# The upper adjacency quarters issued from GpSimd's queue instead of ScalarE's

## The chip, the cores and the metric

One core of a Trainium2 chip runs the whole program. The metric is device time in microseconds, lower is better. The engines are TensorE (PE), VectorE (DVE), ScalarE (ACT), GpSimd (POOL) and SyncE (SP); each works through its own instructions in order, and semaphores order them against each other. DMAs are issued from the queues of SyncE, ScalarE and, after the change, GpSimd.

## What is computed

Two graph layers with a residual and a layer norm each, on 10000 nodes with 128 features, all in float32:

```python
h = item_feat @ W_item.T + b_item
x = layernorm(x + relu(adj @ h + x @ W_user.T + b_user))      # adj is 10000 x 10000, 400 MB
Wh = x @ W
e = leaky_relu(Wh @ a[:128] + (Wh @ a[128:]).T, 0.2)
att = softmax(where(adj > 0, e, -9e15), axis=1)
x = layernorm(x + elu(att @ Wh))
```

## The kernel before

**Two parts.** The first part reads the adjacency once, 400 MB, computes layer 1 and stores the signs of the adjacency as one bit each (`mask_scratch`). The second part computes layer 2 from the bits. The change is in the first part, up to about 1650 us.

**Tiling of the first part.** The 10000 rows are 19 blocks of 512 (`IB`) and a last one of 272; `k` counts them. The 10000 columns are 10 chunks (`NC`) of 1024 (`JC`), the last of 784; `c` counts them. A chunk of a block is loaded in two halves of 256 rows (n = 2c and 2c + 1), so a block has 20 halves. A half lies in one of five slots (`RAW`) of the buffer `raw`: the 128 partitions are four quarters `a` of 32 (`Q`), each with 256 of the 1024 columns, and partition i of a quarter holds rows i, 32 + i, 64 + i and so on. A DMA fills one quarter of one half: 32 partitions x 8 rows x 1 KiB, 256 KB. So a half takes four DMAs and a block 80.

**Who does what with it.** SyncE issues quarters 0 and 1 (`load_half`, L356), ScalarE quarters 2 and 3 (`load_upper`, L979). Both wait for the same count of `half_turned`, the transpose that frees the slot five halves back, and both raise `adj_loaded[slot]`. VectorE waits for all four quarters and transposes the half into `adj_t` (`half_transposed`, L691). When both halves of a chunk are turned, TensorE contracts it with eight matmuls of 512 columns (`contract`, L573), and ScalarE takes the sign (`mask_chunk`, L1011), which VectorE packs by eights (L736, L742, L750). `adj_t` has two chunks, so VectorE may be at most two chunks ahead of TensorE.

**ScalarE's order before.** For each chunk of a block: `loads_ahead` issues the upper quarters of halves 2c + 5 and 2c + 6, then `mask_chunk(c)`; between them, at fixed chunks, come the small steps of the block before: relu (L1032), the copy of x (L1038), deviations (L1045), the store of x1 (L1050), the copy of x1 (L1058), scores (L1068) and their store, which writes single words (L1072), and the mask stores (L1017). Before the first block ScalarE turns the item features (L992) and issues the first upper quarters at chunks 5, 7 and 9 of that loop and behind it.

**GpSimd's order before.** Constants at the start, then one copy per block (`keep_x1`, L458), which waits for ScalarE's copy of x1 (`x1_turned_sb`). In the second part it computes an epilogue per block (L295, L307).

**Loops.** Blocks 0 to 2 are written out, blocks from 3 on run in a hardware loop of two blocks a turn, the last ones are written out again.

Of the kernel before, what the change touches and what calls it, by code (L numbers as in the profile page):

```python
# [50 lines left out]
def resnorm_two_graph_layers(nc, x, adj, item, w_item, b_item, w_user, b_user, w_att, a_att, out):  # L51
# [25 lines left out]
    def cols_of(c):  # L77
        return JA if c < NC - 1 else LJ

    with ExitStack() as ctx:  # L80
# [3 lines left out]
        def sem(name):  # L84
            return ctx.enter_context(nc.semaphore(name))
# [94 lines left out]
        padding_cleared = sem("padding_cleared")  # L180
        adj_loaded = [sem(f"adj_loaded{i}") for i in range(RAW)]
        half_turned = sem("half_turned")
        chunk_contracted = sem("chunk_contracted")
# [250 lines left out]
        def _(pool):  # L434
# [16 lines left out]
            last_chunk = x1_t[:, (NC - 1) * JC:NC * JC]  # L451

            def keep_x1(k, par, width, first):

# [14 lines left out]

            blocks(pool, keep_x1)  # L470
            pool.wait_ge(x1_plain_made, 2)
# [196 lines left out]
        def _(dve):  # L668
# [7 lines left out]
            def half_transposed(k, n, width):  # L676

                c, half, slot = n // 2, n % 2, n % RAW
                steps = steps_of(c)
                groups = HG if half == 0 or width == IB else width // Q - HG  # L680
                off = 0 if c < NC - 1 else LOFF

                uses = k * (2 * NC // RAW) + n // RAW + 1
                dve.wait_ge(adj_loaded[slot], uses * (16 * A))
                if half == 0 and not (isinstance(k, int) and k * NC + c < 2):
                    dve.wait_ge(chunk_contracted, k * NC + c - 1)
                    dve.wait_ge(mask_made, k * NC + c - 1)
# [272 lines left out]
        def _(act):  # L960
            def load_upper(k, n, width):

                c, half = n // 2, n % 2
                slot = n % RAW
                groups = HG if half == 0 or width == IB else width // Q - HG
                rows = Q if half == 0 or width == IB else TAIL - HG * Q - (groups - 1) * Q
                off = 0 if c < NC - 1 else LOFF
                if not (isinstance(k, int) and k * 2 * NC + n < RAW):
                    act.wait_ge(half_turned, k * (2 * NC) + n - RAW + 1)
                for a in (2, 3):  # L970
                    cols = slice(c * JC + a * cols_of(c), c * JC + (a + 1) * cols_of(c))
                    if rows == Q:
                        src = adj[bass.ds(k * IB + half * HG * Q, groups * Q), cols].rearrange("(g i) w -> i g w", i=Q)
                        dst = raw[a * Q:(a + 1) * Q, slot, 0:groups, off:off + cols_of(c)]
                    else:
                        assert groups == 1
                        src = adj[N - rows:N, cols]
                        dst = raw[a * Q:a * Q + rows, slot, 0, off:off + cols_of(c)]
                    act.dma_start(dst, src).then_inc(adj_loaded[slot], 16)  # L979

            for c in range(NC):
                n = min(N, (c + 1) * JC) - c * JC
                if c >= 5 and (c - 5) // 2 < RAW and c % 2 == 1:
                    load_upper(0, (c - 5) // 2, IB)
                act.wait_ge(item_turned, c + 1)
# [15 lines left out]

            for n in range(NC // 2 - 2, RAW):
                load_upper(0, n, IB)

            def mask_chunk(k, c, width):
# [7 lines left out]
            def store_masks(k, half, width):  # L1013
# [4 lines left out]
                              packed[:, half, 0:HC * width // 4]).then_inc(masks_stored[half], 16)  # L1018

            def loads_ahead(k, c, nxt):  # L1020

                for n in (2 * c + RAW, 2 * c + 1 + RAW):
                    if n < 2 * NC:
                        load_upper(k, n, IB if nxt else TW)
                    elif nxt:
                        load_upper(k + 1, n - 2 * NC, nxt)

# [45 lines left out]

            def layer1(k, par, width, first, nxt=IB):
# [22 lines left out]

            layer1(0, 0, IB, True)
            layer1(1, 1, IB, False)
            layer1(2, 0, IB, False)  # L1100
            with act.Fori(3, NB - 3, 2) as k:
                layer1(k, 1, IB, False)
                layer1(k + 1, 0, IB, False)
            layer1(NB - 2, 1, IB, False)
            layer1(NB - 1, 0, IB, False, TW)
            layer1(NB, 1, TW, False, 0)

# [104 lines left out]
```

## Time and profile before

| | us |
|---|---|
| three runs | 3139.74, 3150.01, 3197.87 |
| median | 3150.01 |
| the profiled execution | 3156.98 |
| its span in the trace | 3155.2 |

The profile is one execution. Its page gives busy time and instructions of each engine, the same in 40 slices of the span (79 us each), the DMA queues, the chain of work that ended last (followed back from the last instruction, at each step to what released it), and the costliest groups of instructions by line. PE and DVE overlap, so their shares don't add. "q1" is SyncE's DMA queue and "q10" ScalarE's. ACTq, SPq and POOLq mean the queue of the engine: issuing a DMA, arithmetic on registers. "issue" is time in which an engine waited for nothing that the profile shows. A line such as L979 is the line of the kernel that made the instruction. The DMA share of a window can exceed 1, since packets of one engine overlap.

### The profile page before, as it was taken

The page shows a single profiled execution, that of the slowest core. Times are in us where ns is not written, and L with a number is a line of the kernel's source. Part 1 is how long each engine was busy: PE and PEld are TensorE (multiplying, and loading weights), DVE is VectorE, ACT ScalarE, POOL GpSimd, SP SyncE. Part 2 cuts the span into 40 slices and gives each one's busy share as a digit, 9 for nine tenths or more (in the row PEclk, how much of TensorE's full clock was granted, in tenths as well). Part 3 has the DMA queues.
Part 4 walks back from the last instruction along what each step waited for, and adds up shares of the span by engine and source line. Part 5 has one row for each costly group of instructions (what it writes and reads, how often), then busy time and mean ns, then how long its engine had stood idle before and what let it go on. Part 6 is the DMA issues. An engine that isn't in the chain of part 4 may idle for free.

```text
span 3155.2 us, 50455 instructions
## 1 busy us (share of the span) xinstructions
PE 2947.8 (93%) x16484; PEld 2121.8 (67%) x16484; DVE 2646.8 (84%) x3522; ACT 861.7 (27%) x506; POOL 246.6 (8%) x186
## 2 busy tenths in 40 slices
PE   8999998888997889899997999999999999999998
PEld 5444443343443334344477999999999999999995
DVE  5888876676775677677779999999999999999995
ACT  3555444344443344444441100000000000000000
POOL 0000000000000000000003111112111111111120
PEclk9999999999999999899998999999999999999999
DMA  9999999999999999999971000000000000000000
GB/s 268 314 302 300 286 272 247 233 250 246 277 271 217 230 263 270 237 275 271 264 176 60 12 19 21 19 15 15 18 15 15 15 15 15 15 23 15 15 7 9
DMA packets 498749, 457.98 MB, mean 145 GB/s; under 512 B 39744, under 2 KB 490992, under 8 KB 498544
## 3 DMA queue, kind: packets, MB, share of 16 engines
q1 hardware_dynamic: 248352, 233.87, 30.2%
q10 hardware_dynamic: 250320, 223.28, 29.1%
q8 instruction: 24, 0.39, 0.1%
q14 instruction: 53, 0.43, 0.1%
HBM read 433.81 MB, written 23.22 MB: 145 GB/s over the span
## 4 chain that ended last, share of the span: by engine, by line
PE 60%; DMA 18%; ACTq 8%; DVE 8%; issue 4%; ACT 1%; DVEq 0%; SPq 0%
PE bank L631 42%; DMA area<-in_adj_dram 18%; PE bank L573 17%; ACTq L979 7%; DVE area L691 3%; DVE area_s L844 2%; DVE unpacked L902 1%; PE bank L598 0%; ACTq L1017 0%; DMA area_x<-in_L_gnn_item_feat_dram 0%; ACT area_m L1011 0%; PE bank L510 0%; PE bank L552 0%; ACT area L1123 0%; DVEq L924 0%
## 5 line engine op out<-in xcount | busy, mean ns | idle before, releaser
L631 PE MATMUL bank<-area_h,area_s 128*128 (+2 forms) x12482 | 1443.6, 277 | 47.2 <-DVE area_s L844 47.2
L573 PE MATMUL bank<-area,area_h 128*128 128x512 f32 (+1 forms) x3160 | 1396.9, 600 | 86.0 <-DVE area L691 85.5
L631 PEld LDWEIGHTS bank<-area_h,area_s 128*128 128x128 f32 (+1 forms) x12482 | 1405.9, 191 | 83.6 <-issue 72.0
L691 DVE STREAM_TRANSPOSE area<-area 128x2048 f32<-128x2048 f32 (+3 forms) x400 | 894.1, 2235 | 376.9 <-DMA area<-in_adj_dram 270.3
L844 DVE SCALAR_TENSOR_TENSOR area_s<-area,c_col,unpacked 128x512 f32<-128x512 uint8 (+2 forms) x1580 | 1170.3, 801 | 37.9 <-PE bank L631 26.2
L573 PEld LDWEIGHTS bank<-area,area_h 128*128 128x128 f32 x3160 | 609.8, 196 | 817.2 <-issue 719.5
L1011 ACT ACTIVATE area_m<-area 128x4096 uint8<-128x4096 f32 (+1 forms) x200 | 700.1, 3501 | 853.5 <-issue 582.4
L1171 ACT ACTIVATE std_o<-mv,eps_col 128x4 f32<-128x4 f32 (+1 forms) x20 | 6.0, 298 | 929.2 <-DVE mv L869 929.2
L902 DVE TENSOR_TENSOR unpacked<-area,bit_of 128x1024 uint32<-128x1024 uint32 (+1 forms) x200 | 246.1, 1231 | 0.0
L736 DVE SCALAR_TENSOR_TENSOR packing<-area_m 128x512 uint32<-128x512 uint32 (+1 forms) x200 | 134.0, 670 | 38.6 <-ACT area_m L1011 38.5
L458 POOL COPY area_x<-area_s 128x512 f32 (+1 forms) x19 | 11.7, 613 | 1603.8 <-ACT area_s L1058 1603.8
L295 POOL TENSOR_TENSOR area<-wh_mean,den 128x512 f32<-128x512 f32 x19 | 19.8, 1042 | 1158.8 <-DVE den L857 1158.8
L742 DVE SCALAR_TENSOR_TENSOR packing<-packing 128x256 uint32<-128x256 uint32 (+1 forms) x200 | 75.3, 377 | 0.0
L1158 ACT COPY area<-bank 128x258 f32<-128x258 f32 (+1 forms) x40 | 12.9, 375 | 210.1 <-PE bank L631 210.1
L1164 ACT ACTIVATE area<-area 128x512 f32<-128x512 f32 (+1 forms) x20 | 12.5, 625 | 172.9 <-POOL area L307 171.0
L750 DVE SCALAR_TENSOR_TENSOR packed<-packing 128x128 uint32<-128x128 uint32 (+1 forms) x200 | 49.7, 249 | 0.1
L552 PEld LDWEIGHTS bank<-w_ts,area_s 128*128 128x128 f32 (+1 forms) x158 | 23.5, 220 | 35.1 <-ACT area_s L1058 30.4
L552 PE MATMUL bank<-w_ts,area_s 128*128 128x2 f32 (+1 forms) x158 | 23.1, 267 | 23.5 <-ACT area_s L1058 23.5
L535 PE MATMUL bank<-ident,area_s 128*128 128x128 f32 (+1 forms) x79 | 14.3, 309 | 27.8 <-DVE area_s L695 27.7
L307 POOL TENSOR_SCALAR area<-area 128x512 f32<-128x512 f32 x19 | 38.2, 2012 | 0.0
L535 PEld LDWEIGHTS bank<-ident,area_s 128*128 128x128 f32 (+1 forms) x79 | 9.9, 153 | 41.0 <-DVE area_s L695 39.6
L1113 ACT COPY area_h<-bank 128x387 f32<-128x387 f32 (+1 forms) x27 | 12.6, 474 | 88.9 <-PE bank L598 88.9
(102 smaller groups left out, 674.3 us busy)
## 6 DMA issues: line engine op xcount, KB each, us to landing
area<-in_adj_dram SPq DMA_DIRECT2D x702, 256.0 KB, 8.3
area<-in_adj_dram ACTq DMA_DIRECT2D x702, 256.0 KB, 10.5
area<-in_adj_dram SPq DMA_DIRECT2D x78, 196.0 KB, 6.9
area<-in_adj_dram ACTq DMA_DIRECT2D x78, 196.0 KB, 8.4
mask_scratch<-packed ACTq DMA_DIRECT2D x38, 320.0 KB, 13.1
area<-mask_scratch SPq DMA_DIRECT2D x19, 640.0 KB, 3.9
x_scratch<-area_s ACTq DMA_DIRECT2D x20, 256.0 KB, 14.6
area<-x_scratch SPq DMA_DIRECT2D x20, 256.0 KB, 2.8
```

Of the source, the lines that this page charges most:

```text
L307: ops.tensor_scalar(el[:, 2, 0:w], el[:, 0, 0:w], 0.0, -1.0, ALU.max, ALU.add).then_inc(elu_halves, 1)
L552: mm = nc.tensor.matmul(ps_ts[0:m, 2 * t:2 * t + 2], x1_blk[:, t * P:t * P + m], w_ts[:, :], start=True, stop=True)
L573: mm = nc.tensor.matmul(acc[par][:, 0:width], h[:, c * SPC + s, :], adj_t[:, c % 2, s * width:(s + 1) * width], start=(c == 0 and s == 0), ...
L631: mm = nc.tensor.matmul(bank[0:m, (t % 2) * DEN:(t % 2 + 1) * DEN], prob[:, slot, t * P:t * P + m], right, start=start and t % 2 == 0, sto ...
L691: nc.vector.transpose(dst, src).then_inc(half_turned, 1)
L736: nc.vector.scalar_tensor_tensor(out=packs[:, 0:4, 0:w], in0=m[:, 0:4, :], scalar=4, in1=m[:, 4:8, :], op0=ALU.logical_shift_left, op1=ALU ...
L742: nc.vector.scalar_tensor_tensor(out=packs[:, 4:6, 0:w], in0=packs[:, 0:2, 0:w], scalar=2, in1=packs[:, 2:4, 0:w], op0=ALU.logical_shift_l ...
L750: nc.vector.scalar_tensor_tensor(out=packed[:, c // HC, (c % HC) * w:(c % HC + 1) * w], in0=packs[:, 4, 0:w], scalar=1, in1=packs[:, 5, 0: ...
L844: nc.vector.scalar_tensor_tensor(out=prob[:, slot, 0:width], in0=lhs, scalar=scalar, in1=mask, op0=ALU.max, op1=ALU.mult).then_inc(weights ...
L902: nc.vector.tensor_tensor(unpacked[:, slot, 0:n, 0:w], src.bitcast(U32)[:, None, :].to_broadcast([P, n, w]), bit_of[:, 0:n, None].to_broad ...
L979: act.dma_start(dst, src).then_inc(adj_loaded[slot], 16)
L1011: nc.scalar.activation(mask_out[:, c % 2, 0:w], adj_t[:, c % 2, 0:w], ACT.Sign).then_inc(mask_made, 1)
```

## The change

`load_upper` and `loads_ahead` move from ScalarE's program to GpSimd's. GpSimd now walks through the blocks chunk by chunk: two halves' upper quarters, and the copy of x1 of the block before at chunk 6. The first five halves wait for the item chunks (`item_turned` 2, 4 and 6 for halves 0, 1 and 2). The upper quarters raise a semaphore of their own, `upper_loaded[slot]`, and VectorE waits for both. ScalarE's walk loses `loads_ahead` and nothing else.

```diff
+        upper_loaded = [sem(f"upper_loaded{i}") for i in range(RAW)]
...
+            def load_upper(k, n, width):
...
+                if not (isinstance(k, int) and k * 2 * NC + n < RAW):
+                    pool.wait_ge(half_turned, k * (2 * NC) + n - RAW + 1)
+                for a in (2, 3):
...
+                    pool.dma_start(dst, src).then_inc(upper_loaded[slot], 16)
...
-            blocks(pool, keep_x1)
+            def layer1(k, par, width, nxt=IB):
+                first = isinstance(k, int) and k == 0
+                for c in range(NC):
+                    loads_ahead(k, c, nxt)
+                    if c == at(6) and not first:
+                        keep_x1(k - 1, 1 - par, IB, False)
+
+            for n in range(RAW):
+                if n < NC // 2 - 2:
+                    pool.wait_ge(item_turned, 2 * n + 2)
+                load_upper(0, n, IB)
+            layer1(0, 0, IB)
...
+            with pool.Fori(3, NB - 3, 2) as k:
+                layer1(k, 1, IB)
+                layer1(k + 1, 0, IB)
...
+            keep_x1(NB, 1, TW, False)
...
-                dve.wait_ge(adj_loaded[slot], uses * (16 * A))
+                dve.wait_ge(adj_loaded[slot], uses * 32)
+                dve.wait_ge(upper_loaded[slot], uses * 32)
...
-            def load_upper(k, n, width):
...
-                    act.dma_start(dst, src).then_inc(adj_loaded[slot], 16)
...
-                if c >= 5 and (c - 5) // 2 < RAW and c % 2 == 1:
-                    load_upper(0, (c - 5) // 2, IB)
...
-            for n in range(NC // 2 - 2, RAW):
-                load_upper(0, n, IB)
...
-                    loads_ahead(k, c, nxt)
...
+            blocks(act, layer1)
```

## Rows read from the trace of the kernel before

**Rows 1.** The page: rate in 40 slices, adjacency transposes, ScalarE's issues.

```profile
GB/s 268 314 302 300 286 272 247 233 250 246 277 271 217 230 263 270 237 275 271 264 176 60 12 19 21 19 15 15 18 15 15 15 15 15 15 23 15 15 7 9
...
L691 DVE STREAM_TRANSPOSE area<-area 128x2048 f32<-128x2048 f32 (+3 forms) x400 | 894.1, 2235 | 376.9 <-DMA area<-in_adj_dram 270.3
...
area<-in_adj_dram ACTq DMA_DIRECT2D x702, 256.0 KB, 10.5
```

**Rows 2.** The page: the chain that ended last, by line.

```profile
PE bank L631 42%; DMA area<-in_adj_dram 18%; PE bank L573 17%; ACTq L979 7%; DVE area L691 3%; DVE area_s L844 2%; DVE unpacked L902 1%; PE bank L598 0%; ACTq L1017 0%; DMA area_x<-in_L_gnn_item_feat_dram 0%; ACT area_m L1011 0%; PE bank L510 0%; PE bank L552 0%; ACT area L1123 0%; DVEq L924 0%
```

**Rows 3.** Windows: stretch, length, busy us by engine, TensorE clock, DMA share, GB/s.

```profile
110.00:366.00 256.00, 256.00 (x651) 117.10 (x651) 216.50 (x244) 137.47 (x57) 1.87 (x3) 1.00 1.10 308
...
1000.00:1500.00 500.00, 449.12 (x1070) 201.12 (x1069) 356.75 (x391) 221.50 (x89) 3.67 (x6) 0.95 1.10 256
```

**Rows 4.** GpSimd in order of time: start, length, line, operation, idle before.

```profile
153.34 0.63 POOL L458 COPY area_x<-area_s 128x512 f32<-128x512 f32 x1 [149.75 <-ACT area_s L1058]
...
366.59 0.61 POOL L458 COPY area_x<-area_s 128x512 f32 x1 [70.15 <-ACT area_s L1058]
449.28 0.61 POOL L458 COPY area_x<-area_s 128x512 f32 x1 [82.08 <-ACT area_s L1058]
...
1562.41 0.61 POOL L458 COPY area_x<-area_s 128x512 f32 x1 [79.71 <-ACT area_s L1058]
```

**Rows 5.** Chain by line, from 200 to 400, then 1000 to 1100 us.

```profile
by line: PE bank L573 87.8%; DMA area<-in_adj_dram 8.3%; PE bank L571 1.3%; PE bank L552 1.2%; DVE area L691 1.0%; issue 0.7%; PE bank L543 0.7%; PE bank L535 0.5%; PE bank L561 0.4%; DVE packing L736 0.3%; ACTq L979 0.3%
...
by line: DMA area<-in_adj_dram 70.3%; ACTq L979 22.3%; DVE area L691 7.0%; issue 5.7%; ACTq L1017 1.9%; ACTq L1050 1.6%; ACTq L1072 0.5%; ACT area_m L1011 0.2%; ACTq L969 0.2%; ACT ts_col L1068 0.2%; ACTq L1008 0.1%; ACTq L1006 0.1%; ACTq L
```

**Rows 6.** Waits (total, times, longest), 110 to 360, then 500 to 1500 us.

```profile
DVE area L691 <- DMA area<-in_adj_dram: 2.1, 4, 1.3
...
DVE area L691 <- DMA area<-in_adj_dram: 221.8, 138, 6.4
```

**Rows 7.** Source lines: L979 110 to 360, L979 and L356 500 to 1500.

```profile
L979 ACTq DMA_DIRECT2D area<-in_adj_dram x142: 317/384/3231, 111.1 to 359.2; - x142
...
DMA to landing us min/median/max: 4.5/9.3/14.8
...
L979 ACTq DMA_DIRECT2D area<-in_adj_dram x467: 318/1287/6768, 502.5 to 1496.6; - x156
...
  DVE area L691: 218.5, 133
...
DMA to landing us min/median/max: 4.3/11.8/20.5
...
L356 SPq FUSED_REGOPS  x470: 37/37/51, 500.9 to 1499.5; - x157
...
L356 SPq DMA_DIRECT2D area<-in_adj_dram x470: 316/317/4917, 501.1 to 1499.7; - x157
...
  DVE area L691: 4.5, 4
...
DMA to landing us min/median/max: 4.4/8.1/18.8
```

**Rows 8.** DMA queues in the microsecond from 1010, then from 852.

```profile
DMA packets 230, 0.23 MB, mean 228 GB/s; under 512 B 14, under 2 KB 229, under 8 KB 229
...
q1 hardware_dynamic: 17, 0.02, 8.4%
...
DMA packets 364, 0.35 MB, mean 352 GB/s; under 512 B 20, under 2 KB 364, under 8 KB 364
...
q1 hardware_dynamic: 179, 0.17, 53.6%
```

**Rows 9.** Source lines L295 and L307.

```profile
L295 POOL TENSOR_TENSOR area<-wh_mean,den x19: 1041/1041/1043, 1764.3 to 3069.0; 128x512 f32<-128x512 f32 x19
...
L307 POOL TENSOR_SCALAR area<-area x19: 1977/2013/2017, 1770.2 to 3074.3; 128x512 f32<-128x512 f32 x19
```

**Rows 10.** TensorE in order of time: the first contraction.

```profile
43.98 7.13 PE L573 MATMUL bank<-area,area_h 128*128 128x512 f32 x16 [1.29 <-DVE area L691]
```

More of the change, by code:

```diff
@@ L451, in _, with loads_ahead @@
             last_chunk = x1_t[:, (NC - 1) * JC:NC * JC]
+            def load_upper(k, n, width):
+                c, half = n // 2, n % 2
+                slot = n % RAW
+                groups = HG if half == 0 or width == IB else width // Q - HG
+                rows = Q if half == 0 or width == IB else TAIL - HG * Q - (groups - 1) * Q
+                off = 0 if c < NC - 1 else LOFF
+                if not (isinstance(k, int) and k * 2 * NC + n < RAW):
+                    pool.wait_ge(half_turned, k * (2 * NC) + n - RAW + 1)
+                for a in (2, 3):
+                    cols = slice(c * JC + a * cols_of(c), c * JC + (a + 1) * cols_of(c))
+                    if rows == Q:
+                        src = adj[bass.ds(k * IB + half * HG * Q, groups * Q), cols].rearrange("(g i) w -> i g w", i=Q)
+                        dst = raw[a * Q:(a + 1) * Q, slot, 0:groups, off:off + cols_of(c)]
+                    else:
+                        assert groups == 1
+                        src = adj[N - rows:N, cols]
+                        dst = raw[a * Q:a * Q + rows, slot, 0, off:off + cols_of(c)]
+                    pool.dma_start(dst, src).then_inc(upper_loaded[slot], 16)
+            def loads_ahead(k, c, nxt):
+                for n in (2 * c + RAW, 2 * c + 1 + RAW):
+                    if n < 2 * NC:
+                        load_upper(k, n, IB if nxt else TW)
+                    elif nxt:
+                        load_upper(k + 1, n - 2 * NC, nxt)
             def keep_x1(k, par, width, first):
@@ L468, in keep_x1 @@
                     nc.gpsimd.tensor_copy(x1_plain[:, IB:IB + width], x1_blk[:, 0:width]).then_inc(x1_kept, 1)
-            blocks(pool, keep_x1)
+            def layer1(k, par, width, nxt=IB):
[9 more added lines that the diff above has]
+            layer1(0, 0, IB)
+            layer1(1, 1, IB)
+            layer1(2, 0, IB)
+            with pool.Fori(3, NB - 3, 2) as k:
+                layer1(k, 1, IB)
+                layer1(k + 1, 0, IB)
+            layer1(NB - 2, 1, IB)
+            layer1(NB - 1, 0, IB, TW)
+            layer1(NB, 1, TW, 0)
+            keep_x1(NB, 1, TW, False)
             pool.wait_ge(x1_plain_made, 2)
@@ L960, in _ @@
         def _(act):
-            def load_upper(k, n, width):
[L963 to L978, printed above, removed]
-                    act.dma_start(dst, src).then_inc(adj_loaded[slot], 16)
             for c in range(NC):
                 n = min(N, (c + 1) * JC) - c * JC
-                if c >= 5 and (c - 5) // 2 < RAW and c % 2 == 1:
-                    load_upper(0, (c - 5) // 2, IB)
                 act.wait_ge(item_turned, c + 1)
@@ L1018, in store_masks @@
                               packed[:, half, 0:HC * width // 4]).then_inc(masks_stored[half], 16)
[L1020 to L1026, printed above, removed]
             def relu(k, par, width):
@@ L1072, in scores_out, with layer1 @@
                     act.dma_start(s_dram[:, bass.ds(k * IB, IB)].rearrange("o (t p w) -> p (o t) w", p=P, w=1), ts_col[:, :, 1:2]).then_inc(s_stored_dram, 16)
-            def layer1(k, par, width, first, nxt=IB):
+            def layer1(k, par, width, first):
                 live = width if width == IB else TAIL
@@ L1096, in layer1 @@
                         store_masks(k, 0, width)
[L1098 to L1106, printed above, removed]
+            blocks(act, layer1)
             def wh_copied(lo, hi):
```

## The prediction

> **What bounds the kernel now.** I read the page first [rows 1, 2]. The kernel has two parts. In the first, up to about 1650 us, the DMA row is full and the adjacency streams in at 210 to 310 GB/s; in the second the rate is about 15 GB/s and TensorE works without a break. The diff touches only the first. In the chain of work that ended last, L631, L844 and L902 are the second part (45% of the span together); what is left is TensorE at L573 (17%), landings of adjacency (18%) and ScalarE's queue issuing L979 (7%). So the first part has two bounds in turn, and the question is when each holds.
>
> The windows say when [rows 3]. From 110 to 366 us TensorE is busy for all 256 us, at full clock, and DMA moves 308 GB/s. From 1000 to 1500 us TensorE is busy for 449 of 500 us, at 0.95 of its clock, and DMA moves 256 GB/s. GpSimd's one copy per block is a ruler for the block period [rows 4]: it makes 19 of them; from the first, at 153.34, to the fourth, at 366.59, a block takes 71.1 us, and from there to the eighteenth, at 1562.41, 85.4 us. The difference is 14.3 us per block, 14 x 14.3 = 201 us in all, and that is all that this change can give back, since the first spell is already bound by TensorE: its chain is 87.8% L573 [rows 5]. In the later spell the chain has no TensorE in it: 70.3% is landings and 22.3% L979 on ScalarE's queue.
>
> Who is late? VectorE's transposes (L691) wait for adjacency 2.1 us in the early 250 us and 221.8 us in the later 1000 us [rows 6]. Of the later wait 218.5 us are owed to DMAs issued by L979, the upper quarters from ScalarE, and 4.5 us to L356, the lower quarters from SyncE [rows 7], though both are asked for by the same semaphore and have the same shape. L979's issue has also grown: median 384 ns early, 1287 ns later, up to 6768 ns, while L356 stays at 317 ns. ScalarE issues four of them per chunk between two mask instructions. Their landing is later too, 11.8 us against 8.1.
>
> The bandwidth is not simply used up. In one microsecond where the upper queue is nearly alone (17 of 230 packets are the lower queue's) 228 GB/s move; in one where the two have equal shares, 352 [rows 8]. The queues feed the two halves of the partitions, and when they take turns instead of overlapping, a third of the rate is lost. A late upper half makes them take turns.
>
> **The change part by part.** (a) *ScalarE loses its adjacency issues*: 780 full-size ones [rows 1] and 20 small ones of the last block. On its queue remain the mask instructions, the stores and the small copies. Nothing of this is on the early chain; in the later spell it is the 22.3%. ScalarE's masks come no later than now.
>
> (b) *GpSimd gains the same 800 issues* and waits for the same count of `half_turned`. What stands before it there: one copy per block (0.61 us, [rows 4]), placed after the loads of chunk 6. It waits for ScalarE's copy of x1, which stands at chunk 5 in ScalarE's own order, before the half that the next load waits for is turned, so I cost it at 0.6 us per block, hidden. If that cover went, the loads of chunk 7 would be late, and L691 behind them.
>
> (c) *The price of one issue on GpSimd*, t, decides the case, and no row shows it: GpSimd issues no DMA in this trace. GpSimd must get through 40 issues per block, so 40t is a third bound beside TensorE's 71.1. Lower end: 0.32 us, the same transfer from SyncE [rows 7]. Upper end: if GpSimd builds the 256 pieces of a transfer (32 partitions x 8 rows of 1 KiB) one by one in software, each on a reading and a writing side, its slowest pass over 512 elements, 2.01 us (L307 [rows 9]), is the nearest row for 512 such steps; with ScalarE's 0.38 us for the issue itself, 2.4 us. Between them I take GpSimd's faster pass over 512 elements, 1.04 us (L295 [rows 9]), plus 0.38: t = 1.4 us, so 40t = 57 us, hidden under TensorE's 71.1. Cover ends at t = 71.1/40 = 1.78 us. A slot of the ring of five lives 5 x 3.55 = 17.8 us at the early pace; less a transpose of 2.2 us [rows 1], 15.6 us are left for two issues (2.8) and a landing (9.3 [rows 7]), 12.1 in all: early enough.
>
> [...]
>
> (d) *The separate semaphore* adds one wait in front of each of 400 transposes. SyncE's register step takes 37 ns [rows 7], so some 40 ns each, 16 us over the kernel, on a VectorE that is busy 216 of 256 us while TensorE is the bound [rows 3]: nothing, and 16 us without that cover.
>
> (e) *The first five halves* go out from the second item chunk on instead of from the sixth. They take bandwidth from the item tiles: 0.5 MB at 308 GB/s is 1.7 us for each of three. Against that, block 0 finds its halves landed. I cost it at 0, with 5 us either way.
>
> **The sum**, on the profiled execution (span 3155.2 us, 3157.0 with what lies around it; the median of the runs is 3150.0, 0.2% lower). Best case: every block takes 71.1 us, 3155 - 201 = 2954. I don't expect all of it. The pace changes between the copies at 366.59 and 449.28 us [rows 4], where the code does nothing new; whatever tips it there can tip a kernel with better ordered loads too. If one block in five still runs at the later pace, 0.2 x 201 = 40 us stay: 2995 us, 5% less than now. Parts (a) to (e) add nothing else.
>
> **The rivals.** *A, the forecast*: punctual upper loads, t below 1.78, most blocks at TensorE's pace: 2995, within 2954 and 3060.
>
> *B, nothing that can be measured*: the 16 DMA engines are one pool, and lateness on L979 is a symptom: its issue takes long because the engines are behind. For it: the DMA share is 1.10 in both spells [rows 3], so the engines have work at all times. Then the queues go on taking turns under another name, and only the issue share is partly won: 3100 to 3170, middle 3140. Against it: that SyncE's twin transfers are almost never waited for. [...] The equal share of 1.10 agrees with it; the step from 228 to 352 GB/s with the mixture of the two queues doesn't.
>
> *C, GpSimd becomes the bound (slower)*: one mechanism, 40t above the present period. If t is above 1.78 every full block takes 40t. There are 14 of them at 85.4 us, and 4.6 from 44 to 366.6 us at 71.1, so the time is 3155 + 14(40t - 85.4) + 4.6(40t - 71.1) = 1632 + 744t. It breaks even at t = 2.05, is 2% slower from 2.13 and 2% faster below 1.96. At the upper end, 2.4, it is 3418. For it: two software issues must fit into every 3.55 us, and GpSimd's slower pass over 512 elements already says 2.4. Against it: only that the faster pass says 1.4. [...]
>
> *D, a third queue upsets the sharing (slower)*: GpSimd's transfers come late in the turn of each DMA engine behind SyncE's, at t far below 1.78. Each block would then run at the one-queue rate: 20.5 MB per block at 228 GB/s is 90 us, 14(90 - 85.4) + 4.6(90 - 71.1) = 151, so 3306.
>
> **How the numbers follow.** A 0.43, B 0.19, C 0.33, D 0.05. C is high because t is a guess between 0.32 and 2.4 with the edges at 1.96 and 2.13. Of C, 0.04 falls between these edges. Faster by over 2% (below 3087): 0.43. Within 2%, which is about what a measurement of this kernel tells from no change: 0.19 + 0.04 = 0.23. Slower (over 3213): 0.29 + 0.05 = 0.34. The time is that of A, 2995. The range reaches from the full gain, 2950, to C's upper end, 3420; above it I leave some 0.12 for a t beyond 2.4, below it 0.02. Both signs are inside; A's own range is 2954 to 3060.
>
> **What the profile after would show.** For A: full blocks at 71 to 75 us by GpSimd's copies, L691's wait for adjacency small for both queues, TensorE's clock near 1.0, over 290 GB/s. For B: periods of 83 to 86 us, and the wait of L691 as large as before but owed to GpSimd's line. For C: the GpSimd queue issuing without a gap from the first block, the issues two by two per transpose, and a constant block period of 40 times their mean, in the early blocks too. For D: short issues on GpSimd but landings well above 12 us. The forecast is wrong if the mean issue is above 1.78 us, or if L979's slowness was a symptom; (b) is wrong if the copy's wait has a load queued behind it that VectorE waits for; (e) if TensorE's L573 begins more than 5 us from 44 us [rows 10].

## The result and the profile after

| | us |
|---|---|
| after, three runs | 3406.12, 3406.65, 3409.51 |
| after, median | 3406.65 |
| span of the profiled execution | 3407.8 |
| before, median | 3150.01 |
| ratio after to before | 1.0835, 95% interval 1.0791 to 1.0879 |

The change makes the kernel 8% slower: 252.6 us from span to span. The ratios here and below leave out runs that are over 1.5% slower than the fastest of the same kernel (here 3197.87 us of the kernel before). These lines of the page of the kernel after answer to [rows 1, 2]: rate in 40 slices (now 85 us each), the queues (packets, MB, share of 16 engines' span), the chain that ended last, two groups of instructions, and the issues with their median time to landing. L741 is now the adjacency transpose, L472 GpSimd's load, L357 SyncE's, L622 the contraction, L487 GpSimd's copy of x1.

```profile
GB/s 219 243 231 232 228 235 232 239 236 219 224 217 229 224 232 214 235 230 231 226 229 224 89 12 14 14 22 17 17 14 14 17 21 14 17 14 14 18 9 8
...
q1 hardware_dynamic: 248352, 233.87, 34.0%
q0 software_dynamic: 61792, 200.05, 25.1%
...
PE bank L680 38%; DMA area<-in_adj_dram 34%; SPq L357 7%; DVE area L741 4%; PE bank L622 4%; DVE area_s L894 3%; DVE unpacked L952 1%; SPq L365 1%; DMA area_x<-in_L_gnn_item_feat_dram 1%; PE bank L647 0%; DVE packing L786 0%; PE bank L559 0%; ACT area L1131 0%; PE bank L584 0%; PE bank L550 0%
...
L741 DVE STREAM_TRANSPOSE area<-area 128x2048 f32<-128x2048 f32 (+3 forms) x400 | 894.5, 2237 | 653.2 <-DMA area<-in_adj_dram 568.3
...
L472 POOL DMA_DIRECT2D area<-in_adj_dram x800 | 466.8, 585 | 1390.2 <-DVE area L741 1276.8
```

The 300 GB/s of the early slices are gone; it is about 230 from the first slice to the end of the first part. In the chain the contraction has shrunk from 17% to 4%, landings have grown from 18% to 34%, and the issue queue in it is no longer ScalarE's (L979, 7%) but SyncE's (L357, 7%), a line the change did not touch. The transposes wait 568.3 us for adjacency, before 270.3. And q0, GpSimd's queue, moves 200 MB in 61792 packets: for the full transfers it puts four 1-KiB pieces into one packet of 4096 bytes (44928 such packets, 64 for each of 702 transfers; 12800 of the rest are of 4 bytes), where q1 has one packet for each piece (180000 of 1024 bytes).

The windows of the kernel after (stretch, length, busy us by engine, TensorE's granted clock, DMA share, GB/s; compare [rows 3]) and GpSimd's copies of x1, the 1st, 4th and 18th (compare [rows 4]):

```profile
110.00:366.00 256.00, 215.12 (x493) 95.18 (x494) 165.68 (x187) 106.18 (x42) 66.32 (x114) 0.92 1.08 234
...
1000.00:1500.00 500.00, 408.56 (x940) 180.81 (x939) 315.79 (x350) 195.46 (x79) 124.94 (x213) 0.91 1.07 227
```
```profile
193.37 0.62 POOL L487 COPY area_x<-area_s 128x512 f32<-128x512 f32 x1
...
471.09 0.62 POOL L487 COPY area_x<-area_s 128x512 f32 x1
...
1807.39 0.62 POOL L487 COPY area_x<-area_s 128x512 f32<-128x512 f32 x1
```

The first copy comes 40.0 us later than before, the next three blocks take 92.6 us each in place of 71.1 (+64.5), the next fourteen 95.5 in place of 85.4 (+140.5): 245 of the 252.6 us. So both spells of before are lost, the fast one more: even in the early window TensorE is busy for only 215 of 256 us. Of the first 40 us, 12.3 are the start (point e below).

The waits from 500 to 1500 us (compare [rows 6]), and the two loading lines in that stretch (duration ns min/median/max; compare [rows 7]), first SyncE's, then GpSimd's:

```profile
DVE area L741 <- DMA area<-in_adj_dram: 328.4, 127, 12.2
```
```profile
L357 SPq DMA_DIRECT2D area<-in_adj_dram x420: 316/786/12421, 498.9 to 1496.3; - x140
...
  DVE area L741: 325.0, 128
...
DMA to landing us min/median/max: 4.8/15.1/26.4
...
L472 POOL DMA_DIRECT2D area<-in_adj_dram x416: 586/586/600, 510.3 to 1496.9; - x139
...
DMA to landing us min/median/max: 5.3/8.7/16.2
```

The roles are swapped. Before, the upper quarters were waited for (218.5 us) and SyncE's hardly (4.5). Now SyncE's are waited for (325.0 us) and GpSimd's never. GpSimd's issue is short and steady, 0.586 us; it spends its time waiting for slots. It is SyncE's issue that has grown, 317 to 786 ns at the median and up to 12.4 us, and its landing is 15.1 us. One microsecond of the kernel after, from 1015, by queue (compare [rows 8]):

```profile
DMA packets 126, 0.25 MB, mean 253 GB/s; under 512 B 5, under 2 KB 84, under 8 KB 126
...
q0 software_dynamic: 46, 0.17, 68.7%
q1 hardware_dynamic: 80, 0.08, 36.4%
```

Both queues have work, and GpSimd's gets twice the bytes in fewer packets. By the program its packets go to the upper 64 partitions alone.

### The profile page after: what moved, and what is told of

It is laid out like the page before. It is cut to its first block, busy times and chain, and to the rows that moved or that the text cites. A ratio compares the mean times of both kernels' runs of the same rounds, so it can differ in the third digit from the quotient of the medians.

```text
span 3407.8 us, 50976 instructions
## 1 busy us (share of the span) xinstructions
PE 3022.4 (89%) x16484; PEld 2143.3 (63%) x16484; DVE 2648.7 (78%) x3522; ACT 861.8 (25%) x506; POOL 712.1 (21%) x986
## 3 DMA queue, kind: packets, MB, share of 16 engines
q0 software_dynamic: 61792, 200.05, 25.1%
## 4 chain that ended last, share of the span: by engine, by line
PE 43%; DMA 35%; DVE 10%; SPq 8%; issue 4%; ACT 1%; DVEq 0%; POOL 0%; ACTq 0%
PE bank L680 38%; DMA area<-in_adj_dram 34%; SPq L357 7%; DVE area L741 4%; PE bank L622 4%; DVE area_s L894 3%; DVE unpacked L952 1%; SPq L365 1%; DMA area_x<-in_L_gnn_item_feat_dram 1%; PE bank L647 0%; DVE packing L786 0%; PE bank L559 0%; ACT area L1131 0%; PE bank L584 0%; PE bank L550 0%
## 5 line engine op out<-in xcount | busy, mean ns | idle before, releaser
L622 PE MATMUL bank<-area,area_h 128*128 128x512 f32 (+1 forms) x3160 | 1470.0, 624 | 238.4 <-DVE area L741 238.1
L741 DVE STREAM_TRANSPOSE area<-area 128x2048 f32<-128x2048 f32 (+3 forms) x400 | 894.5, 2237 | 653.2 <-DMA area<-in_adj_dram 568.3
L622 PEld LDWEIGHTS bank<-area,area_h 128*128 128x128 f32 x3160 | 632.3, 204 | 1022.3 <-issue 783.9
L472 POOL DMA_DIRECT2D area<-in_adj_dram x800 | 466.8, 585 | 1390.2 <-DVE area L741 1276.8
L1172 ACT ACTIVATE area<-area 128x512 f32<-128x512 f32 (+1 forms) x20 | 12.5, 625 | 172.4 <-POOL area L308 170.5
L308 POOL TENSOR_SCALAR area<-area 128x512 f32<-128x512 f32 x19 | 38.2, 2011 | 0.0
L304 POOL TENSOR_SCALAR area<-area 128x512 f32<-128x512 f32 x19 | 32.8, 1727 | 3.1 <-POOL area L301 3.1
L819 DVE TENSOR_TENSOR area_h<-bank,b_item_row 128x512 f32<-128x512 f32 (+1 forms) x20 | 12.7, 677 | 26.3 <-PE bank L559 26.3
```

The lines of the kernel that those rows point to most:

```text
L308: ops.tensor_scalar(el[:, 2, 0:w], el[:, 0, 0:w], 0.0, -1.0, ALU.max, ALU.add).then_inc(elu_halves, 1)
L472: pool.dma_start(dst, src).then_inc(upper_loaded[slot], 16)
L622: mm = nc.tensor.matmul(acc[par][:, 0:width], h[:, c * SPC + s, :], adj_t[:, c % 2, s * width:(s + 1) * width], start=(c == 0 and s == 0), ...
```

## The experiments

In the order of the argument: first what makes the kernel after slow (e1 to e6, e11, e12), then what the later spell of before is (e7 to e10, e13). Ratios are to the kernel before, run beside each; its medians there were 3122 to 3148 us.

### Which partitions each queue fills (e1, e2, e3)

The first idea was that at each instant the two queues crowd into the same half of the partitions, so that giving each queue one quarter of either half would mend it. e1 crosses the quarters in the kernel after, e2 in the kernel before (the diff: SyncE's loop, then that of `load_upper`); e3 swaps the halves in the kernel after, SyncE (2, 3) and GpSimd (0, 1).

```diff
-                for a in (0, 1):
+                for a in (0, 2):
...
-                for a in (2, 3):
+                for a in (3, 1):
```

> The changed kernel, with one thing more: SyncE loads quarters 0 and 2, GpSimd 3 and 1, so each queue fills both halves of the partitions, and when the two are in step they write different halves. Theory 1 (ports and turns): a queue that fills 64 partitions can't pass some 210 GB/s, and GpSimd's 4096-byte packets take four times as much per turn as SyncE's 1024-byte ones, so the halves are filled one after the other. Crossing the quarters lifts the limit: TensorE's pace, 71 to 75 us per block, 2950 to 3050 us in all. Theory 2 (the software path is slow in itself, wherever it writes): nothing changes, 3350 to 3450 us.

> The kernel before, with SyncE loading quarters 0 and 2 and ScalarE 3 and 1. Theory 1: the later spell of 85 us per block goes too, since there the two queues also took turns on the halves: 2950 to 3000 us. Theory 2, under which the later spell came from ScalarE issuing late: 3100 to 3170 us, as before.

> The changed kernel with the halves swapped: SyncE loads quarters 2 and 3, GpSimd 0 and 1. Theory 1: no change, 3390 to 3430 us, and it is again SyncE's transfers that land late (15 us against 9). Theory 3 (the place matters: the upper partitions, or the place where GpSimd's descriptors lie): over 2% away from 3407, or GpSimd's transfers late.

e1: 3391.85 us, ratio 1.0875 (1.0776 to 1.0973). e2: 3324.22 us, ratio 1.0675 (1.0605 to 1.0746). e3: 3377.05 us in one run; GpSimd's landing 8.7 us and SyncE's 14.6, though SyncE now fills the upper half. So lateness goes with the queue and not with the place. The time of e3 is 13 us under the range of theory 1 and far from that of theory 3. Crossing doesn't mend the kernel after, against theory 1, and it spoils the kernel before, which neither theory had, in its early spell too:

```profile
110.00:366.00 256.00, 225.03 (x526) 100.17 (x525) 176.79 (x194) 113.06 (x45) 1.98 (x3) 0.94 1.11 254
```

(e2's window.) One queue on each half of the partitions is thus worth something, and the kernel after keeps that and loses it all the same.

### The loads alone (e4)

No computation: VectorE only frees the slots. Seven stages of 40 halves each, with the sources, slots and waits of the kernel:

```diff
+    STAGES = (
+        ("sp", (0, 1), None, ()),
+        ("sp", (0, 1), "act", (2, 3)),
+        ("sp", (0, 1), "pool", (2, 3)),
+        ("sp", (0, 2), "act", (3, 1)),
+        ("sp", (0, 2), "pool", (3, 1)),
+        ("sp", (), "pool", (2, 3)),
+        ("sp", (0, 2, 1, 3), None, ()),
+    )
```

> Leaves out the whole computation: seven stages of 40 halves each are loaded into a ring of five slots, VectorE reads each half once it has landed (about 2.2 us) and frees the slot; in the end x is copied to the output. Stages: SyncE 0,1 alone; SyncE 0,1 with ScalarE 2,3; SyncE 0,1 with GpSimd 2,3; SyncE 0,2 with ScalarE 3,1; SyncE 0,2 with GpSimd 3,1; GpSimd 2,3 alone; SyncE 0,2,1,3 alone. Theory 1: alone and on 64 partitions either queue gives 200 to 212 GB/s; SyncE with GpSimd on separate halves 225 to 250; the crossed pairs over 300. Theory 2: GpSimd alone well below SyncE alone (under 180), and the crossed pair with GpSimd no better than the separate one.

Its windows, one for each stage in that order (VectorE, GpSimd, clock, DMA share, GB/s):

```profile
18.00:103.00 85.00, 77.18 (x34) 0.00 (x0) 1.00 1.12 207
128.00:230.00 102.00, 77.06 (x34) 0.00 (x0) 1.00 1.09 343
263.00:402.00 139.00, 77.15 (x34) 35.80 (x62) 1.00 1.07 250
432.00:565.00 133.00, 76.88 (x34) 0.00 (x0) 1.00 1.12 263
600.00:743.00 143.00, 76.54 (x34) 35.89 (x62) 1.00 1.07 242
764.00:850.00 86.00, 76.68 (x34) 35.68 (x62) 1.00 1.03 203
882.00:1034.00 152.00, 77.72 (x34) 0.00 (x0) 1.00 1.14 239
```

Into 64 partitions either queue alone moves 203 to 207 GB/s: GpSimd's is as fast as SyncE's. Two hardware queues on the two halves reach 343, SyncE with GpSimd 250. The loss is there without any computation, and only in the pair, against theory 2, which had GpSimd alone under 180. But theory 1 had the crossed pairs over 300, and they move 263 and 242. So a limit of 64 partitions and turns between the queues isn't all of it. Why two hardware queues with equal packets move 343 on a half each and 263 crossed was not taken apart. The DMA share is above 1 in all seven stages, while the rate goes from 203 to 343: it tells that the engines have packets, not how much they move.

How the pair shares the engines stands in the packets themselves. One microsecond of the third stage, from 270, and one four later, from 274:

```profile
DMA packets 131, 0.26 MB, mean 262 GB/s; under 512 B 19, under 2 KB 83, under 8 KB 131
q0 software_dynamic: 64, 0.20, 74.1%
q1 hardware_dynamic: 67, 0.07, 29.7%
...
DMA packets 221, 0.21 MB, mean 212 GB/s; under 512 B 14, under 2 KB 221, under 8 KB 221
q1 hardware_dynamic: 221, 0.21, 111.3%
```

In the first microsecond, where both have work, they get about the same number of packets, 64 and 67, so GpSimd gets about three times the bytes (not four, since 19 of these packets have under 512 bytes). In the second GpSimd's part of a half is in, and SyncE moves the rest of its own alone at 212 GB/s, near the 207 of 64 partitions alone.

### The size of the pieces (e5)

If a DMA engine takes one packet from each queue in turn, as the equal counts above suggest, GpSimd's packet of 4096 bytes against SyncE's of 1024 gives the upper half 4/5 of what moves and the lower half 1/5. The halves are then filled one after the other, each near the 205 GB/s of 64 partitions, in place of both at once. e5 varies only the contiguous piece (KiB):

```diff
+        {"sp": ((0, 1), 1), "pool": ((2, 3), 1)},
+        {"sp": ((0, 1), 4), "pool": ((2, 3), 4)},
+        {"sp": ((0, 1), 4), "act": ((2, 3), 4)},
+        {"sp": ((0, 1), 4), "pool": ((2, 3), 1)},
+        {"sp": ((0, 1), 1), "act": ((2, 3), 4)},
+        {"sp": ((0, 1), 2), "pool": ((2, 3), 1)},
+        {"sp": ((0, 1), 1), "act": ((2,), 1), "pool": ((3,), 1)},
```

> Leaves out the whole computation, as the loads alone: seven stages of 40 halves, lower quarters by SyncE, upper ones by another queue, with contiguous pieces of 1, 2 or 4 KiB. Theory 1 in its present form (each DMA engine takes one packet from each queue in turn, and the 64-partition halves are filled evenly only if the packets are of one size): (1) SyncE 1 with GpSimd 1 KiB pieces, sent as 4096-byte packets: 249 GB/s as before; (2) SyncE 4, GpSimd 4: over 300; (3) SyncE 4, ScalarE 4: over 300; (4) SyncE 4, GpSimd 1: over 300; (5) SyncE 1, ScalarE 4, no software queue at all: 225 to 260; (6) SyncE 2, GpSimd 1: 260 to 290; (7) SyncE 1, ScalarE quarter 2, GpSimd quarter 3: 250 to 290. Theory 4 (a software queue disturbs the others whatever its packets): 2 and 4 stay near 250, and 5 is near 340.

```profile
32.00:172.00 140.00, 76.37 (x34) 35.15 (x61) 1.00 1.05 246
200.00:310.00 110.00, 76.89 (x34) 31.54 (x61) 1.00 1.03 316
338.00:451.00 113.00, 77.11 (x34) 0.00 (x0) 1.00 1.02 310
481.00:603.00 122.00, 76.13 (x34) 34.74 (x60) 1.00 1.03 284
637.00:773.00 136.00, 76.56 (x34) 0.00 (x0) 1.00 1.07 252
805.00:928.00 123.00, 76.29 (x34) 34.75 (x60) 1.00 1.04 276
961.00:1088.00 127.00, 76.03 (x34) 17.51 (x30) 1.00 1.11 274
```

The first, second and fifth lines decide. With 4-KiB pieces on both, SyncE and GpSimd reach 316, as much as two hardware queues with them (310). With 1 KiB on SyncE and 4 KiB on ScalarE, no software queue anywhere, it is 252. In its microsecond from 645 the two queues have 62 and 63 packets with 0.06 and 0.22 MB, the same sharing as GpSimd's. With loads alone it is the unequal packets that cost most of the rate, not the software queue. Not all: the fourth line has packets of 4096 bytes on both queues too, but GpSimd's are put together from 1-KiB pieces, and it moves 284, where over 300 was expected and the second line has 316. The median such packet of GpSimd takes 245 ns there and 207 ns in the second.

### Half of GpSimd's part back on ScalarE (e6)

```diff
-                for a in (2, 3):      # ScalarE's load_upper
+                for a in (2,):
...
+                for a in (3,):        # GpSimd's load_upper
```

> The changed kernel with quarter 2 back on ScalarE, so GpSimd loads one quarter of four. Theory 1: while GpSimd has work its packets take most of each turn, but for half as long: a block between 78 and 88 us, 3100 to 3300 us, between the two kernels, with SyncE's transfers landing later than 10 us. Theory 4: nearer to the changed kernel, 3300 to 3400 us.

3250.07 us, ratio 1.0441 (1.0265 to 1.0617), 256 GB/s from 110 to 366 us, 85.6 us a block over its first three and 86.8 over the next fourteen, SyncE's landing 13.9 us: all as theory 1 had it. Half the bytes in long packets cost about half, within a wide interval.

### Equal packets in the kernel after, unequal ones in the kernel before (e11, e12)

Here the piece size is changed inside the real kernels. e11 is the kernel after with 4-KiB pieces on both queues, e12 the kernel before with them on ScalarE's alone.

```diff
+                    if c < NC - 1 and groups == HG:
+                        src = adj[bass.ds(k * IB + (half * HG + 2 * a) * Q, 2 * Q), c * JC:(c + 1) * JC].rearrange("(g i) w -> i g w", i=Q)
+                        dst = raw[a * Q:(a + 1) * Q, slot, :, :].rearrange("p (g u) w -> p g (u w)", u=4)[:, :, 0:4 * JA]
```

> The kernel after, with the full halves of both queues in pieces of 4 KiB: each quarter takes 64 rows of the whole chunk in place of 256 rows of a quarter of it, the same 256 KB. The adjacency then lies wrong in the buffer, so the values are not those of the layers; every instruction and every byte is as in the kernel after, but for a few small memsets at the start. Theory 1 (a DMA engine takes one packet of each queue in turn, and only the unequal size, 1024 against 4096 bytes, starves SyncE's half): equal packets, at least 290 GB/s in the early blocks, landings within 2 us of each other, a block in 71 to 86 us, 2950 to 3200 us in all. Theory 4 (the software queue disturbs the other in itself): still about 230 GB/s and 90 us or more a block, 3300 to 3450 us.

> The kernel before, where only ScalarE's full halves come in pieces of 4 KiB (64 rows of a whole chunk for each quarter) and SyncE's stay at 1 KiB. The upper adjacency lies wrong in the buffer, so the values are not those of the layers. No software queue is used. Theory 1 (unequal packets): the slowness of the kernel after appears without GpSimd: about 230 to 255 GB/s from the first block on, 85 to 95 us a block, SyncE's landing later than ScalarE's, 3280 to 3420 us. Theory 4 (the software queue itself): like before, 3100 to 3200 us.

e11: 3185.38 us, ratio 1.0152 (1.0063 to 1.0242). e12: 3308.76 us, ratio 1.0559 (1.0462 to 1.0655). Windows from 110 and from 1000 us, first e11, then e12:

```profile
110.00:366.00 256.00, 244.06 (x611) 110.34 (x610) 201.97 (x220) 128.91 (x52) 73.96 (x140) 0.99 1.04 289
1000.00:1500.00 500.00, 421.02 (x998) 186.26 (x997) 335.10 (x371) 209.01 (x84) 122.50 (x229) 0.92 1.04 243
```
```profile
110.00:366.00 256.00, 220.83 (x527) 98.48 (x526) 174.52 (x192) 111.51 (x45) 1.98 (x3) 0.94 1.08 247
1000.00:1500.00 500.00, 420.50 (x982) 187.27 (x981) 327.88 (x358) 205.40 (x83) 3.04 (x5) 0.91 1.07 238
```

Equal packets bring the early blocks of the kernel after back to 289 GB/s; unequal ones take the early blocks of the kernel before down to 247, on hardware queues alone. With e13 (below) this makes a square:

| ratio to before | upper half on ScalarE | on GpSimd |
|---|---|---|
| packets equal | 0.9863 (e13, both 4 KiB) | 1.0152 (e11) |
| packets 1024 and 4096 bytes | 1.0559 (e12) | 1.0835 (after) |

Down a column, the unequal packets cost 0.070 and 0.068; along a row, GpSimd's queue costs 0.029 and 0.028. Each ratio is good to about 0.01, so that the two costs add is seen to within 0.02. The upper row has long pieces on both queues. From the kernel before itself, with 1 KiB on both, the way to the kernel after is 0.056 by unequal packets (e12) and 0.028 more by GpSimd's queue.

What makes up the 0.028 (its own 0.53 to 0.59 us an issue, a later start, packets put together from short pieces, or something else in the queue) was not taken apart. By GpSimd's copies e11 takes 74.9 us a block over its first three and 86.1 over the next fourteen, e13 78.0 and 77.7, so between these two it lies in the later spell; its first copy is 11.2 us later, of 111.8 us from span to span. Between the kernel after and e12 (88.6 and 90.2 us a block) it is 4.0 us a block early and 5.3 later. And equal packets don't make SyncE punctual beside GpSimd: in e11 its transfers land after 12.5 us (110 to 360 us) and 13.4 us (500 to 1500 us) at the median, against 10.1 for GpSimd's, more than the 2 us expected, and from 500 to 1500 us VectorE waits 230.3 us for them and 46.3 for GpSimd's.

The expectation of e12 also had SyncE's landing late. Its waits from 500 to 1500 us, first for SyncE's loads (L356), then for ScalarE's (L996):

```profile
L356 SPq DMA_DIRECT2D area<-in_adj_dram x443: 316/781/10305, 499.9 to 1498.0; - x148
...
  DVE area L705: 194.9, 89
...
L996 ACTq DMA_DIRECT2D area<-in_adj_dram x444: 322/352/5385, 499.9 to 1498.5; - x148
...
  DVE area L705: 122.9, 63
```

SyncE's issue grows as in the kernel after, with no GpSimd in it, and its landing is the later one from 110 to 360 us (12.0 against 9.5 at the median). But from 500 us on the landings are alike (8.4 and 8.3), and ScalarE's are waited for too, where GpSimd's in the kernel after never were. So e12 has the loss, and the roles less clearly. One caution more: its upper half reads its rows from other places of the adjacency than that of the kernel after.

### The later spell of the kernel before (e7, e8, e10, e9, e13)

The prediction lived on the drop from 71.1 to 85.4 us a block. Four suspects, one at a time. e7: the three stores of ScalarE go out from GpSimd. e8: the store of the scores writes rows of 512 bytes in place of single words. e10: ScalarE's mask instruction works on 64 columns of 4096. e9: the loads alone on two hardware queues, over 342 halves, with nothing else.

One line of each, in the order e7 (the store of x1; the others alike), e8, e10, e9:

```diff
-                act.dma_start(x1_dram[bass.ds(k * IB, IB), :].rearrange("(t p) d -> p t d", p=P), x1_rows[:, :, :]).then_inc(x1_stored_dram, 16)
+                pool.dma_start(x1_dram[bass.ds(k * IB, IB), :].rearrange("(t p) d -> p t d", p=P), x1_rows[:, :, :]).then_inc(x1_stored_dram, 16)
...
-                    act.dma_start(s_dram[:, bass.ds(k * IB, IB)].rearrange("o (t p w) -> p (o t) w", p=P, w=1), ts_col[:, :, 1:2]).then_inc(s_stored_dram, 16)
+                    act.dma_start(s_dram[:, bass.ds(k * IB, IB)].rearrange("o (t p) -> o t p", p=P), ones[0:1, None, :].to_broadcast([1, TPB, P])).then_inc(s_stored_dram, 16)
...
-                nc.scalar.activation(mask_out[:, c % 2, 0:w], adj_t[:, c % 2, 0:w], ACT.Sign).then_inc(mask_made, 1)
+                nc.scalar.activation(mask_out[:, c % 2, 0:64], adj_t[:, c % 2, 0:64], ACT.Sign).then_inc(mask_made, 1)
...
+        ("sp", (0, 1), "act", (2, 3)),
```

> The kernel before, its adjacency loads where they were, but the stores of masks, x1 and scores issued from GpSimd instead of ScalarE. Theory 5 (the later spell of 85 us per block comes from the stores in ScalarE's ring, which take turns from its adjacency loads until the two halves no longer overlap): TensorE's pace to the end, 2950 to 3050 us. Theory 6 (the spell has nothing to do with where the stores are queued): 3080 to 3170 us, as before.

> The kernel before, but the scores' store to memory is replaced by one of the same size from a row of constants, so 4 pieces of 512 bytes instead of 512 single words; the scores that the second part reads are left out by this. Theory 7 (the single-word writes stall the adjacency reads once per block and throw the queues out of step): the later spell goes, 2950 to 3030 us. Theory 6: 3080 to 3170 us.

> The kernel before, but the mask instruction on ScalarE takes 64 of its 4096 columns, so the masks that are packed and stored are not the adjacency's; this leaves 3.5 us of ScalarE's work per chunk out. Theory 8 (ScalarE's late issues keep the later spell going): ScalarE is free between issues, the spell goes, 2950 to 3030 us. Theory 9: 3080 to 3170 us.

> Leaves out the whole computation, as the loads alone, but one stage only: SyncE 0,1 with ScalarE 2,3, 342 halves, all 19 full blocks but for their last chunk. If the later spell of the kernel before belongs to the memory or to the two queues by themselves (theory 9), the rate falls from 341 to some 250 GB/s after the first few hundred us. If it comes from what else ScalarE and the stores do in the kernel (theory 8), it stays at 330 to 345 GB/s to the end, about 1060 us in all.

> The kernel before, with the full halves of both queues in pieces of 4 KiB, so that the values are not those of the layers. Asked is the later spell of before, 85 us a block from 370 us on. If that spell comes of the two queues falling out of step packet by packet while their pieces are short, it shrinks: under 78 us a block, 2950 to 3060 us. If it comes from what else runs in the layer (stores, waits on ScalarE's own queue), it stays: 83 to 88 us a block, 3090 to 3200 us.

e7: 3092.34, 3118.55, 3232.23 and 3233.80 us, ratio 0.9976 (0.9782 to 1.0171), which is of the first two; its profile is of the last and isn't used here. e8: 3139.52 us, ratio 1.0060 (0.9906 to 1.0214). e10: 3189.94 us, ratio 1.0214 (1.0020 to 1.0408), above both its ranges. None of the three reaches the 2950 to 3050 us of a kernel without the spell, and from 1000 to 1500 us e8 and e10 move 258 and 241 GB/s. In e8 the spell comes later: its first seven blocks take 70.2 to 73.8 us by GpSimd's copies and the eighth 89.0, where before has three of 71 and then 82.7. It is one execution, so whether the single-word stores bring the spell forward isn't known. Nor is it one pace: the fourteen blocks that average 85.4 us in the kernel before take 69.4 to 94.1. e9 keeps 3.03 us a half (61 us a block) to its end; its window:

```profile
500.00:1000.00 500.00, 375.77 (x165) 0.00 (x0) 1.00 1.10 346
```

So neither the memory nor the two hardware queues slow down by themselves. e13 is the kernel before with 4-KiB pieces on both queues: 3084.01 us, ratio 0.9863 (0.9784 to 0.9943).

```profile
110.00:366.00 256.00, 237.40 (x591) 107.56 (x590) 195.01 (x212) 124.95 (x50) 1.94 (x3) 0.97 1.04 284
1000.00:1500.00 500.00, 473.00 (x1172) 215.23 (x1171) 386.47 (x425) 243.49 (x99) 4.27 (x7) 0.97 1.04 280
```

Here there is no second spell: 78.0 us a block over its first three, 77.7 over the next fourteen, as expected if it came from short pieces, though the time is above the 2950 to 3060 us of that answer. The early blocks are slower than with 1-KiB pieces (78.0 against 71.1), the later ones faster (77.7 against 85.4). So the spell hangs on the short pieces together with the rest of the kernel. What tips it over after the fourth block stays open.

## Why the prediction failed

**The reading of before** held as far as it went: two spells, an upper half that lands late, 201 us at stake, and a rate that depends on whether the two queues run side by side. In e4 the same 128 partitions get 343 GB/s from two queues side by side and 239 from SyncE's queue alone.

**(a) ScalarE's issues** left its queue without harm, and what they were in the chain (7%) came back as SyncE's (7%). That answers the question of rival B, whether L979's long issue was a symptom: it was, though the result is not B's (3100 to 3170 us). The prediction took the late upper issues for the cause. L357's issue grew from 317 to 786 ns in the kernel after, and to 781 in e12, with SyncE's program unchanged. In the kernel before, the kernel after and e12 the long issue (1287, 786 and 781 ns) was that of the queue that VectorE waited for most from 500 to 1500 us (218.5, 325.0 and 194.9 us). It doesn't follow every lateness: in e11 SyncE's median is 317 ns while its transfers are late. In e10 ScalarE has little to do between its issues (it is busy for 24 of 500 us from 1000 us on), and the spell stays.

**The step that failed.** The sum's best case, 71.1 us for every block, supposed that punctual upper issues bring overlap, and that "parts (a) to (e) add nothing else". The upper half did become punctual: GpSimd's transfers land after 8.7 us, and VectorE doesn't wait for them in any of the windows from 110 to 360 and from 500 to 1500 us. The overlap went all the same, from 308 to 234 GB/s in the early window and from 256 to 227 in the later one, because the sharing between the two queues changed, a term that the sum put at nothing. GpSimd's packets hold 4096 bytes and SyncE's 1024, they get about equal numbers of packets (64 and 67 in a microsecond of e4), and unequal packets alone, on hardware queues, cost 5.6% (e12); 2.8% more come with GpSimd's queue, from a cause that stays open.

**(b) The copy of x1** on GpSimd: 0.62 us a block, and no row of VectorE waits for L472 from 500 to 1500 us. Right.

**(c) The price of an issue**, taken as 1.4 us between 0.32 and 2.4, is 0.586. 40 issues take 23 us of a block of 95. The term was oversized by 2.4 times, without effect on the forecast's own sum; but it was the ground of rival C. That GpSimd builds the pieces one by one was the author's assumption: a transfer of 256 pieces takes 0.586 us at the median and one of 64 pieces 0.527 (e11). Rival C (0.33) is out: GpSimd waits 1276.8 us for L741, it doesn't issue without a gap. From 500 to 1500 us its issues take 586 to 600 ns.

**(d) The second wait** can't be seen in the trace, and no run measured it alone.

**(e) The start** was costed at 0 with 5 us either way. It is 12.3 us late: TensorE's L622 begins at 56.31 us, before at 43.98 [rows 10].

```profile
45.37 1.97 PE L550 MATMUL bank<-ident,area_x 128*128 128x128 f32 x8 [9.36 <-DMA area_x<-in_L_gnn_item_feat_dram]
...
56.31 19.15 PE L622 MATMUL bank<-area,area_h 128*128 128x512 f32 x44 [1.29 <-DVE area L741]
```

The item tile before that arrives 9.36 us late for TensorE; the longest such wait in that stretch of the kernel before was 1.07 us. The prediction weighed the bytes (1.7 us for each half) and not how SyncE's queue, which also carries the item tiles, fares beside GpSimd's packets. From 20 to 45 us it moves 2.89 MB, before 4.41, and the item tiles issued there land after 16.1 us at the median, before 8.6. That the first upper loads now go out at 14.4 us in place of 23.7 fits this; it wasn't tested alone.

**The rivals.** The measured 3407 us lies inside the stated range, 2950 to 3420, by luck: its upper end is there for C, an issue of 2.4 us, and the issue takes 0.586. What happened is D in its outcome, one-queue rates in both spells: 234 and 227 GB/s and 92.6 to 95.5 us a block, where D said 228 and 90. It had 0.05 of the chance. Its wording had the late side wrong: it made GpSimd's transfers wait behind SyncE's, and its sign, landings on GpSimd well above 12 us, didn't come (8.7; SyncE's are the late ones). So D's near hit is in part luck too. The time that D gave, 3306, is 102 us short of the span; the late start (12.3 us) and the 2.6 and 5.5 us by which a block exceeds 90 (3 x 2.6 + 14 x 5.5 = 85) are 97 of them.

**What was missed in the profile of before.** Packet sizes stood there: in [rows 8] SyncE's 179 packets carry 0.17 MB, so one packet is one 1-KiB piece, and the two queues ran side by side with equal packets. The question to ask of the change was what one packet of the new queue would hold. How two queues with packets of different size share the engines no row of before shows, since its adjacency packets were of one size. e4 shows it: 64 packets of GpSimd's against 67 of SyncE's in a microsecond, and the stages of e5 and the square above follow the packet sizes in the main. What the two halves of the partitions are worth together e4 measures as well: one half alone gets 207 GB/s, both get 343 from two hardware queues with equal packets, and 250 where the packets are unequal, 21% over one half.

**A sum that would have worked.** Take it that, while both queues have work, GpSimd gets four bytes to SyncE's one. GpSimd's 0.52 MB of a half then goes at the 205 GB/s of 64 partitions, 2.56 us, and SyncE gets a quarter of that, 0.13 MB; its other 0.39 MB then goes alone at 206 GB/s, 1.91 us. 4.5 us a half is 89 us a block; measured were 82 (4.1 us a half) with loads alone in e4 and 92.6 to 95.5 in the kernel. It is an estimate, made with the rates of e4 and its near equal counts of packets (64 and 67); in the kernel after, the sharing is less clean (46 packets against 80 in the microsecond shown).

## What to carry to other kernels

Before moving loads to another queue, ask what one packet of each queue will hold. In these runs the queue with 1-KiB packets got too little beside one with packets of 4096 bytes, whichever engine issued the long ones: 250 GB/s with GpSimd (e4) and 252 with ScalarE (e5), where equal packets gave 343 and 310 on two hardware queues and 316 with GpSimd. A growing issue time on a hardware queue didn't name the reason: L979's median went from 384 to 1287 ns inside the kernel before, and after the change it was L357's that stood at 786, in place of 317. A DMA share at 1 says nothing of the rate: it was 1.03 to 1.14 in the stages of e4, at 203 to 343 GB/s. Compare GB/s with that of the same loads run alone.

## What the hardware showed that was not expected

- In the kernel after, GpSimd's queue combines 1-KiB pieces into packets of 4096 bytes (44928 of them), and the 784-byte pieces of the last chunk into packets of six and four (2496 of 4704 bytes, 1248 of 3136); SyncE's queue there makes one packet of each piece (180000 of 1024 bytes, 20000 of 784), and so does ScalarE's in the kernel before (the same counts).
- Where SyncE's and GpSimd's queues both have work they get about equal numbers of packets, not of bytes, in e4 (64 and 67 in a microsecond, with 0.20 and 0.07 MB); it is less clean in the kernel after (46 and 80, with 0.17 and 0.08 MB).
- A GpSimd issue of 256 pieces takes 0.586 us at the median (at most 0.600 from 500 to 1500 us of the kernel after), of 64 pieces 0.527 (at most 0.601 in e11); SyncE's of the same 256 pieces takes 0.317 us at the median from 500 to 1500 us of the kernel before, and 0.786 at the median and up to 12.4 us beside GpSimd's packets in the kernel after.
- Into 64 partitions either queue alone moves 203 to 207 GB/s (e4); two hardware queues with a half each reach 343, one hardware queue on all four quarters 239, two queues crossed 263.
- Long pieces aren't simply better: two hardware queues move 343 GB/s with 1-KiB pieces (e4) and 310 with 4 KiB (e5), alone.
